# Adding expert rows to x through accumulating transfers instead of loads and VectorE additions, in a gated cross-attention and mixture-of-experts kernel

## The reference

```
x = x + tanh(g_xattn) * attention(layernorm(x), ctx_768)      # 16 heads
h = layernorm(x)                                               # 2048 x 256
logits = h @ w_router; two experts of 8 per token, scores = softmax of the two
moe    = sum over the two choices k:  score_k * (silu(p) * g) @ fc2[e_k],  p, g = split(h @ fc1[e_k])
shared = (silu(h @ gate_w) * (h @ up_w)) @ down_w              # hidden width 512
x = x + tanh(g_ffn) * (moe + shared)
```

## Time and profile before

| | |
|---|---|
| three runs | 332.38, 331.18, 331.7 us; median 331.7 |
| span of the profiled execution, first to last instruction | 329.2 us |
| mean granted clock of TensorE | 0.983 |
| TensorE busy | 304.6 us (93%) |
| VectorE busy | 243.6 us (74%) |
| ScalarE busy | 169.2 us (51%) |
| GpSimd busy | 129.8 us (39%) |

### The profile page before, as it was taken

The page is one execution under the profiler, slowest core; times in us unless marked ns, Lnnn a source line. Parts: engine busy times, 40 slices in busy tenths (PEclk is TensorE's granted clock), DMA queues, the critical chain, the costliest instruction groups (busy, mean ns, idle before and its releaser), DMA issues.

```text
span 329.2 us, 8082 instructions
## 1 busy us (share of the span) xinstructions
PE 304.6 (93%) x2505; PEld 244.5 (74%) x2505; DVE 243.6 (74%) x728; ACT 169.2 (51%) x322; POOL 129.8 (39%) x151
## 2 busy tenths in 40 slices
PE   7948889999989979998999989999999999999986
PEld 7627667787768755655465758889988898888875
DVE  4576597798999998687679976666666666633895
ACT  2444767777777744365495236444454444424131
POOL 5732143232465744506760085744333433331000
PEclk9998999999999999996999999999999999999999
DMA  7882776586666362166226112333333333103941
GB/s 232 255 217 80 227 197 207 161 263 193 189 186 177 123 178 84 50 201 250 98 98 164 44 34 83 106 94 108 94 103 98 97 85 111 64 16 133 416 153 64
DMA packets 34069, 47.18 MB, mean 143 GB/s; under 512 B 5519, under 2 KB 27667, under 8 KB 33522
## 3 DMA queue, kind: packets, MB, share of 16 engines
q1 hardware_dynamic: 28706, 34.61, 35.3%
q0 software_dynamic: 4320, 10.92, 9.9%
q10 hardware_dynamic: 1008, 1.18, 1.2%
HBM read 22.20 MB, written 12.62 MB: 106 GB/s over the span
## 4 chain that ended last, share of the span: by engine, by line
PE 41%; DVE 18%; issue 17%; POOL 8%; DMA 7%; SPq 5%; ACT 2%; POOLq 0%; DVEq 0%
PE ps L1744 27%; POOL dispatched L541 4%; DMA stacks<-work 4%; DVE x_all L1334 3%; DVE fc_lo L1177 3%; SPq L381 3%; PE ps L1790 3%; PE ps L1716 2%; PE ps L1562 2%; POOL rs L526 2%; PE ps L1437 1%; SPq L374 1%; DVE fc_lo L1183 1%; DMA stacks<-expert_rows 1%; PE ps L1407 1%
## 5 line engine op out<-in xcount | busy, mean ns | idle before, releaser
L597 POOL DMA_INDIRECT expert_rows<-v_s,slot_u x39 | 38.3, 982 | 58.6 <-ACT v_s L867 46.3
L963 DVE TENSOR_REDUCE mx<-ps 128x8 f32<-128x1024 f32 x32 | 39.1, 1223 | 13.0 <-PE ps L1437 12.7
L1284 DVE TENSOR_TENSOR act<-ps,sil 128x256 f32<-128x256 f32 x39 | 16.6, 425 | 29.9 <-ACT sil L860 29.8
L549 POOL TENSOR_TENSOR work<-work 128x512 bf16<-128x512 f32 x16 | 18.5, 1156 | 50.3 <-ACT work L646 50.2
L677 ACT ACTIVATE probs<-ps 128x1024 f32<-128x1024 f32 x32 | 32.7, 1022 | 9.4 <-PE ps L1470 9.4
L860 ACT ACTIVATE sil<-ps 128x256 f32<-128x256 f32 x39 | 15.0, 384 | 41.4 <-PE ps L1744 41.3
L1744 PE MATMUL ps<-fc_hi,xs_hi 128*128 x78 | 34.2, 439 | 1.4 <-DVE xs_lo L1265 1.4
L1744 PE MATMUL ps<-fc_hi,xs_lo 128*128 x78 | 30.7, 394 | 0.0
L1744 PE MATMUL ps<-fc_lo,xs_hi 128*128 x78 | 30.7, 394 | 0.0
L867 ACT ACTIVATE v_s<-ps,wt 128x256 f32<-128x256 f32 x39 | 18.5, 475 | 19.0 <-PE ps L1744 19.0
L1437 PE MATMUL ps<-stacks 96*128 96x128 bf16 x256 | 20.1, 222 | 7.0 <-DVE mx L963 3.3
(11 more groups left out here) (221 smaller groups left out, 828.4 us busy)
## 6 DMA issues: line engine op xcount, KB each, us to landing
stacks<-work SPq DMA_DIRECT2D x75, 128.0 KB, 3.1
xs_in<-dispatched SPq DMA_DIRECT2D x39, 129.0 KB, 2.0
fc_s<-in_fc SPq DMA_DIRECT2D x8, 512.0 KB, 5.2
stacks<-work POOLq DMA_DIRECT2D x18, 128.0 KB, 3.4
ctx_s<-in_ctx_t SPq DMA_DIRECT2D x8, 256.0 KB, 3.7
fc_s<-in_fc SPq DMA_DIRECT2D x8, 256.0 KB, 5.3
stacks<-expert_rows SPq DMA_DIRECT2D x2, 1024.0 KB, 5.8
probs<-expert_rows SPq DMA_DIRECT2D x2, 1024.0 KB, 9.9
```

What stands on the lines that cost most here:

```text
L549: nc.gpsimd.tensor_tensor(out[:, 2, :], rest, out[:, 1, :], ALU.subtract).then_inc(ready, 1)
L597: nc.gpsimd.indirect_dma_start(ys, bass.IndirectOffsetOnAxis(dst_u[:, r:r + 1], 0), y_out[:, r, :], None, bounds_check=2 * T - 1, oob_is_e ...
L963: nc.vector.reduce_max(mx[:, j, 8 * h:8 * h + 8], ps_s, AX_X).then_inc(max_ok[j][h], 1)
L1284: nc.vector.tensor_tensor(act[:, par], ps[:, 2 + par, FI:2 * FI], sil[:, par], ALU.mult).then_inc(act_ok, 1)
```

## The change

The four loads, the places they went to, the eight `add_expert` and the counters `y_half` and `y_added` are gone. GpSimd, when all scatters have landed, issues eight accumulating transfers (`accum_op=ALU.add`), each of one chunk and one choice: it reads 512 rows of 1 KB from `expert_rows` and adds them to four blocks of `x_all` (512 KB). First all four chunks' first choices, then all four chunks' second choices. Both transfers of a chunk count the same semaphore `y_got[c]`; a second choice is issued only when the first one of its chunk has landed (16), and the chunk is complete at 32. sum_and_add(2) and sum_and_add(3) now wait for 32 of their chunk, and so do the stores of chunks 0 to 2.

```
@@ sync
-            for r in range(4):
-                sp.wait_ge(ysc[r], 16 * len(range(r, NT, 4)))
-            for c in range(NCH):
-                sp.dma_start(y_in[c], y_view[:, CH * c:CH * c + CH]).then_inc(y_got[c], 16)
             for c in range(NCH - 1):
-                sp.wait_ge(y_added, c + 1)
+                sp.wait_ge(y_got[c], 32)
                 sp.wait_ge(base_ok, CH * (c + 1))
                 sp.dma_start(out_view[:, CH * c:CH * c + CH, :], x_all[:, CH * c:CH * c + CH, :]).then_inc(out_done, 16)
@@ gpsimd
             expert_steps(pool, scatter)
+
+            def add_choice(c, k):
+
+                if k:
+                    pool.wait_ge(y_got[c], 16)
+                elif c < 2:
+                    pool.wait_ge(base_ok, CH * (c + 1))
+                nc.gpsimd.dma_start(x_all[:, CH * c:CH * c + CH, :], y_view[:, CH * c:CH * c + CH, k, :],
+                                    accum_op=ALU.add).then_inc(y_got[c], 16)
+
+            for r in range(4):
+                pool.wait_ge(ysc[r], 16 * len(range(r, NT, 4)))
+            for k in range(2):
+                for c in range(NCH):
+                    add_choice(c, k)
@@ vector
             for j in range(NJ):
-                if j == NJ - 1:
-                    add_expert(0, 0)
                 product(2, j)
                 low_of_hidden(2, j)
-            add_expert(0, 1)
-            add_expert(1, 0)
-            add_expert(1, 1)
             product(3, 0)
-            add_expert(2, 0)
-            add_expert(2, 1)
-            ve.wait_ge(y_added, 3)
+            ve.wait_ge(y_got[2], 32)
             sum_and_add(2, 2 * CH, sums)
             low_of_hidden(3, 0)
-            product(3, 1)
-            low_of_hidden(3, 1)
-            product(3, 2)
-            add_expert(3, 0)
-            low_of_hidden(3, 2)
-            add_expert(3, 1)
-            product(3, 3)
-            low_of_hidden(3, 3)
-            ve.wait_ge(y_added, NCH)
+            for j in range(1, NJ):
+                product(3, j)
+                low_of_hidden(3, j)
+            ve.wait_ge(y_got[3], 32)
             sum_and_add(3, 3 * CH, sums)
```

More of the change, by code:

```diff
@@ L198, in build_program @@
         st_f = stacks[:, :, :, :, :].rearrange("p s a h t -> p (s a h t)").bitcast(F32)
-        q_f, k_f = st_f[:, 0:8192 // 2], st_f[:, 8192 // 2:8192]
+        k_f = st_f[:, 8192 // 2:8192]
         fc1_hi, fc1_lo = over("fc1_hi", "stacks", [P, 2 * E, 2 * FI]), over("fc1_lo", "fc1_s", [P, 2 * E, 2 * FI])
@@ L215, in build_program @@
         assert start["ctx_s"] + 2 * 4 * 4 * ROW <= start["work"] + 4 * o0
-        p_f = probs[:, :, :, :].rearrange("p a h t -> p (a h t)")
-        y_in = [home[:, 8 * D * r:8 * D * (r + 1)].rearrange("p (t k d) -> p t k d", t=CH, k=2)
-                for home in (q_f, p_f) for r in range(2)]
         hid_1 = v_s[:, :, :, :].rearrange("p a j e -> p (a j) e")
@@ L271, in build_program @@
             tile_in0 tile_in1 tile_in2 tile_in3 xst_done xst_ok h_done silm_ok act_ok actt_done actt_ok y_done y_ok
-            dst_ok ysc0 ysc1 ysc2 ysc3 y_in0 y_in1 y_in2 y_in3 y_half y_added sig_ok out_done
+            dst_ok ysc0 ysc1 ysc2 ysc3 y_in0 y_in1 y_in2 y_in3 sig_ok out_done
             fhi_ok flo_ok high_ok low_ok xlo_ok prod_ok hhi_ok f2hi_ok f2lo_ok ahi_ok""".split()
@@ L310, in build_program @@
         ysc = [S[f"ysc{r}"] for r in range(4)]
-        y_got, y_half = [S[f"y_in{c}"] for c in range(4)], S["y_half"]
+        y_got = [S[f"y_in{c}"] for c in range(4)]
         xst_done, xst_ok, h_done, silm_ok, act_ok = (S["xst_done"], S["xst_ok"], S["h_done"], S["silm_ok"],
@@ L318, in build_program @@
         xlo_ok, prod_ok, hhi_ok = S["xlo_ok"], S["prod_ok"], S["hhi_ok"]
-        y_added, sig_ok, out_done = S["y_added"], S["sig_ok"], S["out_done"]
+        sig_ok, out_done = S["sig_ok"], S["out_done"]
         def held(eng, value):
```

## The result

The changed kernel is slower. In the first comparison its median is 344.01 us (four runs, 341.03 to 345.54) against 331.93 us before (four runs, 331.18 to 332.38): ratio 1.032, 95% interval 1.0278 to 1.0361. In a later comparison of the same two kernels it was 343.92 against 333.86 us, ratio 1.027, interval 1.0233 to 1.0308. The profiled execution took 341.03 us with a span of 339.3 us; it is the shortest of the four, and the other three have spans of 341.7 to 343.8.

What follows compares the result with a forecast made beforehand. TensorE was taken as the bound. Sums of chunk 2 at 322.6, plus 14.1 to the end and 2.5 for the clock, gave span 339.2; 2.5 more gave 341.7 us, range 331 to 356.

Steps and rivals of the forecast that it cites:

- What bounds the kernel: TensorE, busy 93% of the span; its two waits near the end are all the additions cost, at most 1.5 us.
- The seventh transfer: Second transfer of chunk 2, seventh of eight; the sums of chunk 2 wait for it, and it lands near 322.
- X: Start of VectorE's sums of chunk 2: 322.6 us forecast, 314.86 before; the end follows 14.1 us later.
- The price d: Time one accumulating transfer of 0.5 MB adds to the stream: 2.6 us, expected within 2.2 to 3.2.
- GpSimd's descriptors: One reason for the price: writing descriptors of 512 rows keeps GpSimd busy 2.2 to 3.2 us a transfer.
- rival C: Slow descriptors or read-modify-write in the transfers: 3.9 us each gives 350.8 us, 9.6 each near 391; chance 0.19.
- The stores: Stores of chunks 0 and 1 go out in front of the seventh transfer and delay it by 1.8 us.
- The clock: TensorE's clock falls to half in the pause before down(3,0) and slows the matmuls behind it: 2.5 us.
- The sum: Span 339.2 us against 329.2, 10 us slower; time 341.7 us.
- B: Accumulating transfers run at the load's rate, 1.24 to 1.6 us each: 1.5 us gained, 330.2 us; chance 0.12.

Runs made afterwards that it cites:

- the new order: The kernel before with all eight additions kept and VectorE's last products, additions and sums reordered: ratios to before 0.997 and 0.9942, 331.96 us in the second comparison.
- the experiment: The changed kernel with 38 idle matmuls on TensorE ahead of down(3,0), so that it isn't idle in the pause: 344.3 us, ratio to before 1.036.
- the plain copies: The changed kernel with its eight GpSimd transfers as plain copies in runs of 1 KB, the addition left out: ratio to before 1.002.

## Why the prediction was right, point by point

**What bounds the kernel.** Right, with the ceiling a little low. TensorE's two waits were all that the additions cost; I said 1.5 us at most, the traces without additions and with the new order say 1.7. The idle times in the rows, 1.18 and 0.16 us, understate the waits, because they begin at a matmul's modelled end, while matmuls follow each other faster than that (0.23 us apart at 0.39 us each, 0.12 apart at 0.28). From start to start the two waits are 1.34 us (317.17 - 315.60 - 0.23) and 0.31 us (324.62 - 324.19 - 0.12), together 1.65.

**The seventh transfer.** The mechanism was right: the transfer completes chunk 2, and with the sums, down(3,0) and all behind it wait for it. I forecast X, the start of the sums, at 24.8 us behind the last scatter (322.6 - 297.77); it was 26.5 us (323.23 - 296.76). By terms:

| | forecast us | measured us |
|---|---|---|
| last scatter's start to first transfer's start | 2.5 | 3.05 |
| that to first landing | 2.3 + 2.6 = 4.9 | 6.0 |
| six steps | 15.6 | 17.4 |
| stores in front of the seventh | 1.8 | 0 |
| to the start of the sums | 24.8 | 26.5 |

**The price d** was a term mis-sized, 2.6 against 2.90. Of the two reasons I gave, GpSimd's descriptors fell: 512 rows of 1 KB keep it busy for 1.27 us, not 2.2 to 3.2; its time does not grow in proportion to the rows. The rule of the Trainium skill that I set beside the other ("Collectives: The Full Stack", the bandwidth ceiling: a reduce step moves at half the rate of a copy) names the right place, the DMA engines, and gives 2.47; here an accumulation is 1.64 to 1.74 times the plain copy of the same runs, and no run shows that the second read is what it pays for; the rest of the price is the short runs, which I had named only under rival C. That 2.6 came out close to 2.90 is in part luck: one reason gave too much and the other left a term out.

**The stores** cost the seventh nothing. The first was issued at 317.35, behind the fifth landing, and the steps from there to the sixth and seventh are 3.0 and 2.9 us like the others; the stores took 9.7 and 8.2 us to land. The step to the eighth, 4.4 us, did carry some of it. The missing 1.8 us and the steps that were 1.8 us longer cancel; that is luck.

**The clock.** Right in kind, 1.9 us by the experiment against 2.5. The clock fell at about 319.6, 4.6 us into the pause, and came back at 329.8, 4.3 us behind it. For a chunk that is only a little late I wrote that the clock may not fall. With the plain copies it fell behind a wait of 1.98 us, 2.2 us into the pause, and cost 1.5 us; in four other traces with waits of 0.83 to 1.60 us before down(3,0) it did not.

**The sum.** Behind the last scatter I forecast 41.4 us (339.2 - 297.77), it was 42.5, and 42.75 again. That the span came out as 339.3 against 339.2 owes 1 us to an early arrival at the last scatter; the medians of 344.0 and 343.9 show it better, with 341.7 forecast. The 2.5 us that I put on top of the span are not all time around it, though the section on the kernel before has it so: every execution on record is 1.7 to 1.9 us longer than its span, and the rest is that the profiled execution before was shorter than the median.

**The rivals.** B, accumulation at the rate of the load, ended with the first landing times. The anatomy rule of "DMA: Bandwidth & Descriptors" in the Trainium skill, which led to it, gives 1.2 us for half a megabyte. Only the loads' 1.24 meets that; GpSimd's plain copies took 1.45 us a step in runs of 4 KB and 1.77 in runs of 1 KB. C had the right cause in small: the short runs cost 0.3 to 0.4 us a transfer, while its lowest price, 3.9 us, was 1.3 above mine.

## What to carry to other kernels

Before work is taken off an engine, ask whose wait it causes: the waits of the bounding engine that go back to it, from matmul start to matmul start, are the ceiling of the gain (here 1.65 us for 9.7 us of VectorE), and an exchange of places may reach it without any new mechanism. Work that moves into transfers is paid in the transfers, the addition for itself and short runs on top, and a chain of dependent transfers on one buffer also pays its latency; what counts is the landing of the one that the next consumer needs, so find its place in the queue and multiply. When the bounding engine is made to wait for longer than before, add what its clock loses behind the pause.

## What the runs showed of the hardware

- Adding 0.5 MB from memory to on-chip values by a transfer costs about 1.1 us more than copying it, with runs of 1 KB and of 4 KB alike: 2.90 and 2.52 us in a stream. No other size was measured.
- A copy of 0.5 MB in runs of 1 KB takes 1.77 us in a stream, from GpSimd's queue and from SyncE's; in runs of 4 KB 1.45; the loads, in runs of 8 KB and transfers of 1 MB, take 1.24 for each half.
- GpSimd is busy for 0.54, 0.75, 0.86 and 1.27 us with a plain copy in runs of 4 KB and 1 KB, and an accumulating one in runs of 4 KB and 1 KB.
- An accumulating transfer of 0.5 MB with at most one in front of it lands 5.9 to 6.1 us after its start, a plain one of the same runs after 4.1.
- Stores of 0.5 MB issued beside a stream of accumulating transfers landed after 9.7 and 8.2 us (3.5 in the median in the kernel before). The transfers next to land kept their step, and later ones lost theirs: 4.4 us instead of 2.9 in the changed kernel, 3.6 twice instead of 2.5 and 3.8 twice instead of 2.8 in the two kernels with chunk 2 complete as the fourth.
- The granted clock fell to half behind a wait of TensorE of 1.98 us once, for 3.4 us at a cost of 1.5 us; behind waits of 0.83, 0.87, 1.12 and 1.60 us it stayed at 1.00.
- Kernels with the same work up to the last scatter came to it at 296.8 to 303.6 us in different profiled executions, which is more than most effects studied here. Those that came late had lost more of TensorE's clock on the way (5.1 us the early ones, 6.8 to 12.0 the others). No experiment changed that clock, so it isn't shown to be the cause.
